# Ternary rounding moved and clamps cut into quarters, the first channels loaded in halves, and another order at the seam of two fused layers

## The reference

```python
q = x @ Wq.T + bq; k = x @ Wk.T + bk; v = x @ Wv.T + bv        # 16 heads of 16
q = softmax(q, axis=-1)                                       # over a head's 16 channels
k = softmax(k, axis=-2)                                       # over the 1024 tokens
out = q @ (k.T @ v)                                           # per head
x = norm(x + (norm(out) * ln_g + ln_b) @ Wo.T + bo)
scale = 1.0 / clip(mean(abs(w)), 1e-05)
wq = clip(round(w * scale), -1, 1) / scale                    # ternary, for w1 and w2
h = gelu(ln1(x) @ ternary(w1).T + b1)                         # 256 -> 1024
x = norm(x + ln2(h) @ ternary(w2).T + b2)                     # 1024 -> 256
```

## Time and profile before

| What | us |
|---|---|
| Median of 3 runs (range) | 611.45 (609.54 to 611.67) |
| Profiled execution, its own time | 611.89 |
| Its span, first to last instruction | 610.1 |
| TensorE busy in the span | 556.0 |
| VectorE, ScalarE, GpSimd busy | 516.4, 474.4, 392.0 |

### The profile page before, as it was taken

The page is one execution under the profiler, slowest core; times in us unless marked ns, Lnnn a source line. Parts: engine busy times, 40 slices in busy tenths (PEclk is TensorE's granted clock), DMA queues, the critical chain, the costliest instruction groups (busy, mean ns, idle before and its releaser), DMA issues.

```text
span 610.1 us, 10906 instructions
## 1 busy us (share of the span) xinstructions
PE 556.0 (91%) x3584; PEld 505.6 (83%) x3584; DVE 516.4 (85%) x1303; ACT 474.4 (78%) x912; POOL 392.0 (64%) x376
## 2 busy tenths in 40 slices
PE   0789999997999999998969999999999999999990
PEld 0779999887889988888868898888888888888890
DVE  3797879985887988785756899999999999999985
ACT  2253669678687866876687999999999999999983
POOL 0336495968469496735774777677766667666771
PEclk9898999998999999998979999999999999999996
DMA  7432005050070503015010002222222211220002
GB/s 250 144 132 70 0 3 207 1 189 19 6 272 1 208 2 108 32 57 221 2 70 35 2 28 78 71 69 71 70 70 71 64 44 33 71 70 36 35 35 104
DMA packets 10712, 46.53 MB, mean 76 GB/s; under 512 B 1312, under 2 KB 1568, under 8 KB 8352
## 3 DMA queue, kind: packets, MB, share of 16 engines
q1 hardware_dynamic: 10656, 45.83, 20.9%
HBM read 29.02 MB, written 16.81 MB: 75 GB/s over the span
## 4 chain that ended last, share of the span: by engine, by line
PE 54%; DVE 14%; ACT 11%; POOL 10%; issue 7%; DMA 2%; POOLq 0%; SPq 0%; ACTq 0%; DVEq 0%
PE ring L1693 17%; PE qps_sps_aps_then_y L1717 16%; PE qps_sps_aps_then_y L1568 6%; PE qps_sps_aps_then_y L1585 3%; POOL xc_lo L368 3%; PE ring L1510 2%; POOL xt L389 2%; POOL xt_lo L378 2%; PE ring L1635 2%; PE qps_sps_aps_then_y L1489 2%; POOL qw L399 2%; ACT zjunk L631 2%; DVE z L1065 1%; ACT z L639 1%; PE ring L1610 1%
## 5 line engine op out<-in xcount | busy, mean ns | idle before, releaser
L1717 PE MATMUL qps_sps_aps_then_y<-ff_w_over_xc_lo,ff_a_lo_over_qw 128*128 128x258 f32 x512 | 126.4, 283 | 0.0
L1717 PE MATMUL qps_sps_aps_then_y<-ff_w_over_xc_lo,ff_a_hi_over_xc_lo 128*128 128x258 f32 x512 | 126.3, 283 | 0.0
L1693 PE MATMUL ring<-ff_ht_hi_over_qw,t 128*128 128x512 f32 x256 | 106.0, 414 | 1.6 <-DVE ff_a_lo_over_qw L1152 0.8
L1693 PE MATMUL ring<-ff_ht_lo_over_xc_hi,t 128*128 128x512 f32 x256 | 101.3, 396 | 0.0
L1717 PEld LDWEIGHTS qps_sps_aps_then_y<-ff_w_over_xc_lo,ff_a_hi_over_xc_lo 128*128 128x128 f32 x512 | 96.9, 189 | 3.5
L1717 PEld LDWEIGHTS qps_sps_aps_then_y<-ff_w_over_xc_lo,ff_a_lo_over_qw 128*128 128x128 f32 x512 | 96.8, 189 | 3.3
L1152 DVE SCALAR_TENSOR_TENSOR ff_a_lo_over_qw<-ring,ff_rho,ff_a_hi_over_xc_lo 128x512 fp32r<-128x512 f32 x128 | 91.4, 742 | 7.8 <-ACT ff_a_hi_over_xc_lo L697 6.9
L679 ACT ACTIVATE ring<-ring,bias 128x512 f32<-128x512 f32 x128 | 83.9, 675 | 11.2 <-PE ring L1693 10.1
L474 POOL TENSOR_TENSOR ff_accp_over_xt_lo<-ff_accp_over_xt_lo,ff_sq_over_ek_et_hi 128x512 f32<-128x512 f32 x64 | 84.2, 1316 | 7.2 <-ACT ff_sq_over_ek_et_hi L695 2.7
L695 ACT ACTIVATE ff_sq_over_ek_et_hi<-ring 128x512 f32<-128x512 f32 x128 | 78.7, 615 | 0.5
L697 ACT CAST ff_a_hi_over_xc_lo<-ring 128x512 fp32r<-128x512 f32 x128 | 77.5, 606 | 0.0
(11 more groups left out here) (173 smaller groups left out, 1673.6 us busy)
## 6 DMA issues: line engine op xcount, KB each, us to landing
x_scratch<-z SPq DMA_DIRECT2D x16, 514.0 KB, 2.9
ff_x_over_w_raw_xc<-x_scratch SPq DMA_DIRECT2D x16, 514.0 KB, 4.7
xc<-in_x_chan_dram SPq DMA_DIRECT2D x8, 1024.0 KB, 6.9
xt<-in_x_tok_dram SPq DMA_DIRECT2D x8, 1024.0 KB, 4.9
out_dram<-ff_z_over_et_lo SPq DMA_DIRECT2D x16, 512.0 KB, 3.5
w_raw<-in_w_dram SPq DMA_DIRECT2D x2, 1024.0 KB, 5.8
rows<-in_rows_dram SPq DMA_DIRECT2D x1, 512.0 KB, 4.8
w_raw<-in_wq_dram SPq DMA_DIRECT2D x1, 256.0 KB, 2.7
```

The lines of the kernel that those rows point to most:

```text
L1693: mm = nc.tensor.matmul(ff_bank(k, m), t1[:, c, m * P:(m + 1) * P], h[:, k % 2, c], start=(c == 0 and j == 0), stop=(c == CH - 1 and j == 1))
L1717: last = nc.tensor.matmul(ff_yps[:, t, 0:C + 2], a[:, m % DEPTH, t * P:(t + 1) * P], ff_w2[:, m], start=(m == 0 and j == 0), stop=(m == FC ...
```

## The change

1. **Start.** SyncE's list becomes wq, row bq alone, xc in two halves of 512 tokens (a semaphore each), wk, vectors, wv, wo, then batch 1's channels, and only then the tokens, ident, mask and the other rows. ScalarE splits the halves apart and takes over the high parts of wk, wv, wo and the scalings of `fold_wo`. VectorE makes the low parts; one softmax denominator of batch 0 moves behind the second key maximum. TensorE's queries 0 and 1 wait for the first half alone, and the waits for wv and the masks move to their first users.
2. **Rounding** in steps 2 and 5 moves from after `out_variance(b - 1, 0)` to VectorE's end of the step.
3. **Clamps** in steps 3 and 6 are twelve instructions of 128x512 in place of three of 128x2048, all behind `pt_high(b, 1)`.
4. **Seam.** The lists of all four engines are in another order; TensorE's first pass of the chunk loop is written out with `ff_transposes(1, 1)` between two `attend`.

```diff
         def _(sp):
             sp.dma_start(w_raw[:, 0], wq).then_inc(w_in[0], 16)
+            sp.dma_start(rows[:, 0], rows_d[:, 0]).then_inc(bq_in, 16)
+            for h in range(2):
+                sp.dma_start(xc[:, :, h * HALF:(h + 1) * HALF], x_chan[0][:, :, h * HALF:(h + 1) * HALF]
+                             ).then_inc(first_in[h], 16)
+            sp.dma_start(w_raw[:, 1], wk).then_inc(w_in[1], 16)
             sp.dma_start(vecs[:], vecs_d).then_inc(v_in, 16)
-            sp.dma_start(rows[:], rows_d).then_inc(v_in, 16)
-            sp.dma_start(xc[:], x_chan[0]).then_inc(xc_in, 16)
-            for n, w in ((1, wk), (2, wv), (3, wo)):
+            for n, w in ((2, wv), (3, wo)):
                 sp.dma_start(w_raw[:, n], w).then_inc(w_in[n], 16)
-            sp.dma_start(ident[:], ident_d).then_inc(m_in, 16)
-            sp.dma_start(mask[:], mask_d).then_inc(m_in, 16)
-            sp.dma_start(xt[:, 0], x_tok[0]).then_inc(xt_in[0], 16)
...
             chan_load(1)
+            sp.dma_start(xt[:, 0], x_tok[0]).then_inc(xt_in[0], 16)
+            sp.dma_start(ident[:], ident_d).then_inc(m_in, 16)
+            sp.dma_start(mask[:], mask_d).then_inc(m_in, 16)
+            sp.dma_start(rows[:, 1:], rows_d[:, 1:]).then_inc(rows_in, 16)
...
+            def weight_high(n):
+                act.wait_ge(w_in[n], 16)
+                nc.scalar.copy(w_hi[:, n].rearrange("p a c -> p (a c)"), w_raw[:, n].rearrange("p a c -> p (a c)")
+                               ).then_inc(w_high[n], 1)
...
-            def ternary_top(n):
+            def ternary_top(n, j):
                 act.wait_ge(f_round, n + 1)
-                nc.scalar.activation(f_raw, f_raw, ACT.Relu, bias=tern_bias[:, 0:1], scale=-1.0).then_inc(f_one, 1)
+                nc.scalar.activation(f_quarter(j), f_quarter(j), ACT.Relu, bias=tern_bias[:, 0:1], scale=-1.0
+                                     ).then_inc(f_one, 1)
...
-            chan_hi(0)
+            for h in range(2):
+                half = slice(h * HALF, (h + 1) * HALF)
+                act.wait_ge(first_in[h], 16)
+                nc.scalar.copy(xc_hi[0][:, :, half], xc[:, :, half]).then_inc(first_hi_ok, 1)
+            weight_high(1)
+            weight_high(2)
+            fold_wo()
+            weight_high(3)
             chan_hi(1)
...
-            for c in range(CH):
-                split_lo(xc_lo[0][:, c], xc[:, c], xc_hi[0][:, c]).then_inc(xc_lo_ok, 1)
-            split_weight(1)
+            for h in range(2):
+                half = slice(h * HALF, (h + 1) * HALF)
+                dve.wait_ge(first_hi_ok, h + 1)
+                split_lo(xc_lo[0][:, :, half], xc[:, :, half], xc_hi[0][:, :, half]).then_inc(xc_lo_ok, 1)
+            weight_low(1)
...
-                if b in (2, 5):
-                    ternary_round(b // 5)
                 pt_low(b, 2)
...
                 e_inverse(b)
+                if b in (2, 5):
+                    ternary_round(b // 5)
...
-                if v == 0:
+                if b == 0:
+                    pe.wait_ge(xc_lo_ok, 1 + v // 2)
+                elif v == 0:
                     pe.wait_ge(xc_lo_ok, CH * (b + 1))
...
             pe.wait_ge(w_ready[1], 1)
-            pe.wait_ge(w_ready[2], 1)
-            pe.wait_ge(v_ready, 1)
-            pe.wait_ge(m_in, 32)
...
             state_product(NB - 1)
+            state_transpose(NB - 1)
             ff_first(0, 0)
+            state_project(NB - 1)
             ff_first(0, 1)
-            state_transpose(NB - 1)
             ff_transposes(1, 0)
             ff_first(0, 2)
-            state_project(NB - 1)
```

More of the change, by code:

```diff
@@ L201, in both_halves @@
         xc_in = sem("xc_in")
+        bq_in, rows_in = sem("bq_in"), sem("rows_in")
+        first_in = [sem(f"first_in{h}") for h in range(2)]
+        first_hi_ok = sem("first_hi_ok")
         w_in = [sem(f"w_in{n}") for n in range(4)]
@@ L205, in both_halves @@
         w_scaled = sem("w_scaled")
-        w_hi_ok = sem("w_hi_ok")
+        w_high = [sem(f"w_high{n}") for n in range(4)]
         w_ready = [sem(f"w_ready{n}") for n in range(4)]
@@ L834, in _ @@
             ff_gelu(1, 5)
+            squares(NB - 1, 1)
             ff_gelu(1, 6)
@@ L1401, in _ @@
             ff_ht_low(2, 1)
+            residual(NB - 1, 1)
             ff_hidden_stats(0)
```

208 lines of the change are left out of this document (114 added, 94 removed).

## The result

The change takes 595.61 us (median of 4 runs, 594.69 to 596.41) against 610.88 for the kernel before on the same chip: ratio 0.974, 95% interval 0.970 to 0.977. The prediction was 594.5, range 588 to 601. The profiled execution spans 594.0 us, 16.1 less than before.

The account below looks back on a forecast made before the run. TensorE bounds it, busy 556.0 of 610.1 us; the gain lies in its waits and lower clock. From 611.89: -9.8 -0.7 -4.0 -0.7 -1.7 = -16.9, 595.0; median 0.4 lower, 594.5; range 588 to 601.

Parts of the forecast that it names:

- Part 1, the start: Kernel start to batch 1's first query product: half loads and casts moved to ScalarE gain 9.8 us, ends 7.5 and 12.
- I take 5.8: Start: the first 512 KB half of xc, issued near 1.6 us, lands at 5.8 us, so TensorE starts at 9.4.
- It fits, by 0.8 us: Batch 1's first query product, ready at 23.0 us, needs GpSimd's xc_lo, expected done at 22.2.
- rival (b): Seam waits short enough to keep TensorE's upper clock, 1.7 us per stretch; step 0 gains 1 more; about 590; chance 0.17.
- The port race: Start, wv's low part against GpSimd's xc_lo: VectorE first by 0.15 us; losing costs 2.4 us, about 597, chance 0.20.
- Part 2, the rounding: Steps 2 and 5: waits of 0.99 and 0.94 go, 0.6 each comes back at the next step; net -0.7 us.
- Part 3, the clamps: Twelve smaller ScalarE clamps end TensorE's 2.63 us wait: batch 3 gains 4.0 us, batch 6 gains 0.7.
- xe_hi may come 0.1 to 0.8 late, and 2.8 us of key products cover that: Clamp steps: six quarters, 3.5 us, fill ScalarE's 3.38 idle; xe_hi's delay hides under key products, less 1.3 us.
- Part 4, the seam: Reordered lists from last attention step into feed-forward: -1.0 us, plus the 0.74 wait gone; -1.7 us (+1.5 to -5).
- The other moves: GpSimd's rstd items, squares and normalise of the last batch, inside the feed-forward loop: cost nothing, under TensorE's cover.
- about 1.3 us for the transpose and 2.6 before state_project: Seam: two TensorE waits of these sizes replace two of 2.8 us.

Follow-up runs that it names:

- the second profile of the change: The changed kernel run again unaltered, as the measure for the next three runs: 595.96 us, ratio 0.975 to the kernel before.

## Why the prediction was right, point by point

**Part 1, the start** (-9.8 predicted, -10.1 with the start alone). The sum is right, its pieces are less so, and that they closed is luck in part. "I take 5.8" for the half's landing: ScalarE saw it at 6.99. From there to the first matmul I had 3.6 us; it took 3.75. Hence 10.74 instead of 9.4. What made up for it was the clock: 8.56 us for the four query products where I had kept 9.42; other profiles of the same start have 8.36 to 9.55. The first query product of batch 1 came at 23.51 (predicted 23.0). "It fits, by 0.8 us" was too kind: GpSimd's xc_lo ended at 23.45, and in the second profile of the change TensorE waited 0.18 us for it. The key transposes came 9.4 us earlier (36.79); before, TensorE's timeline has

```profile
46.15 0.33 PE L1610 MATMUL ring<-ident,ek 128*128 128x128 f32 x1 [2.36 <-DVE pt_lo L900]
```

So far VectorE's shorter list brought them, with the wait ahead of them as long as it was. The last 1.1 us of step 0 is the clock behind that wait: from the transposes to the step's end 10.16 us at a mean granted clock of 0.83 before, 9.04 at 1.00 in the change and with the start alone, and again 10.15 at 0.83 in the second profile of the change. I had no term for it in the sum; rival (b) had one for the seam and for the room in step 0, but none for this.

**The port race** was given by 0.15 us to VectorE; in the change's profile it was 0.83, in the kernel with the old seam and the same start -0.08. The mechanism and the loser's price stand: the low part waited 2.2 us (2.4 predicted), and the step became 2.9 longer, 1.2 of it in TensorE's wait and the rest by the lower clock around it. The Trainium skill (SBUF — State Buffer, Who interferes with whom) has it that who issues first keeps the pair for a whole instruction. At the start the traces agree: GpSimd's subtraction 0.08 us ahead makes the low part 2.90 long, and the low part 0.3 us or more ahead takes 0.69. For the last chunk they cannot settle it: `ff_gain` starts 0.03 us ahead of the add in both profiles in which it takes 1.34 or 1.35.

**Part 2, the rounding** (-0.7): steps 2 and 5 gained 1.3 and 1.4, and 0.91 and 0.93 came in before the next state products, where I had written 0.6 each with an end of 1.2. Net -0.9, of which 0.7 in step 5 is rather time that the late step 4 gave back: it is gone where step 4 is not late (w2 behind the stores). The mechanism, the rounding holding GpSimd up, is shown by the run that took it away.

**Part 3, the clamps** (-4.7 for steps 3 and 6): steps 3 and 6 fell by 4.4 and 0.9, and by 5.3 and 1.9 without the rounding's new waits in them. Of the 4.4, 1.6 is the clock after a wait of 2.63, which the unchanged step 3 of the start-only kernel did not show. The step that failed is in "xe_hi may come 0.1 to 0.8 late, and 2.8 us of key products cover that". It came 0.83 after the step's start (before 0.20), and TensorE's cover held. One reason is the size of a quarter: 0.72 to 0.77 us, where I took 0.59 from a cast; the twelve of batch 3 take 8.2 us, the three before took 6.0. But ScalarE's whole list stood behind it: the token load, w2 and the stores went out about 1 us later in their step, into a queue with 3 MB of loads, and step 4 paid 1.5 us. I had priced what is queued behind the late instruction on TensorE alone.

**Part 4, the seam** (-1.7): -1.0 with the seam alone, within about 1 us of clock. "The other moves ... lie in a loop in which TensorE is full; I cost them at nothing" failed: the residual of the last batch ahead of `ff_hidden_stats(0)` costs 1.07 us of waiting in chunk 1 (VectorE is at it from 330.19 to 331.9 and begins `ff_sums` at 332.00; behind the statistics, in the run with w2 behind the stores, `ff_sums` begins at 327.34). A TensorE that is full has no room for a late VectorE either. The two seam waits came out as 1.82 and 1.19 with one of 0.98 between them, in place of "about 1.3 us for the transpose and 2.6 before state_project".

**The sum.** -10.1 -6.2 -1.0 makes -17.3; the change's own profile lost the last chunk's race (+1.3): -16.0, against 16.1 between the spans. So close a sum of single profiles is luck in part: the clock alone moves step 0 by 1.1, step 3 by 1.6 and step 7 by 1.2 us between executions of the same code. What is shown is that each part does in its own steps, alone, what it does in the change. The forecast of 594.5 held with it: it gave the seam 0.7 too much and the clamps with the rounding 0.8 too little, and had no term for the last chunk's race.

## What to carry to other kernels

Before moving a piece on VectorE, list what GpSimd does beside the new place and beside everything that shifts with it; a 128x1 add can cost 2 us. Late work on an engine is covered only if every list behind it is, the DMA queue's stores among them. A half-size first load paid about 2 us at the first key product by itself; the function table loaded ahead of it brought the first matmul forward (9.70 and 10.38, in the change 10.74 and 11.06), but not the first key product (19.25 and 19.50, in the change 19.30 and 19.42).
